# A four-block mixer on one core: ScalarE makes the decays of two token tiles in the even step, with one Exp over both, and the square and high part of z stand in front of them

## The reference, cut to what matters

```python
hBC = silu(conv(proj))                       # x, B and C
dt = softplus(dt + dt_bias)
A_cumsum = cumsum(A * dt)                    # per head, within a chunk
Lmat = exp(segment_sum(Ac))                  # exp(A_cumsum[l] - A_cumsum[s]), 0 above the diagonal
Gm = einsum('bclhn,bcshn->bclsh', C, B)
Y_diag = einsum('bclsh,bcshp->bclhp', Gm * Lmat, x * dt)
...
y = Y_diag + Y_off + D * x
z = y * silu(gate)                           # the norm's root is applied after the sum
out = z * norm_w @ out_proj_w.T
```

## Time and profile before

| what | value |
|---|---|
| median of three executions | 1733.1 us |
| the profiled execution's own time | 1734.61 us |
| its span, first to last instruction | 1732.9 us |
| TensorE busy | 97% |
| VectorE busy | 70% |
| ScalarE busy | 73% |
| GpSimd busy | 44% |
| mean granted TensorE clock | 0.989 of full speed |

### The profile page before, as it was taken

The page is one execution under the profiler, slowest core; times in us unless marked ns, Lnnn a source line. Parts: engine busy times, 40 slices in busy tenths (PEclk is TensorE's granted clock), DMA queues, the critical chain, the costliest instruction groups (busy, mean ns, idle before and its releaser), DMA issues.

```text
span 1732.9 us, 27059 instructions
## 1 busy us (share of the span) xinstructions
PE 1679.2 (97%) x9568; PEld 1388.4 (80%) x9568; DVE 1204.7 (70%) x1846; ACT 1265.2 (73%) x2171; POOL 754.7 (44%) x792
## 2 busy tenths in 40 slices
PE   6998898899999999999999999999999999999999
PEld 4877677788888888888888888888888888888777
DVE  4565685667776677668676767676767676767784
ACT  4332148887888778878888888788887888788851
POOL 3543122444444444544454444444444445345570
PEclk9999999999999999999999999999999999999999
DMA  4310225323233323232423232323233333332311
GB/s 164 116 68 1 73 68 156 102 86 112 86 113 96 109 89 112 87 117 73 127 89 104 75 110 101 102 95 110 88 104 94 110 98 106 93 108 77 107 68 49
DMA packets 98565, 166.47 MB, mean 96 GB/s; under 512 B 11616, under 2 KB 49888, under 8 KB 96768
## 3 DMA queue, kind: packets, MB, share of 16 engines
q1 hardware_dynamic: 98432, 164.75, 29.8%
HBM read 158.43 MB, written 6.29 MB: 95 GB/s over the span
## 4 chain that ended last, share of the span: by engine, by line
PE 80%; DVE 5%; ACT 2%; issue 1%; DVEq 0%; ACTq 0%
PE bank L210 14%; PE bank L212 14%; PE bank L211 14%; PE bank L1949 7%; PE bank L1950 7%; PE bank L1915 7%; PE bank L1953 7%; PE bank L1935 4%; PE bank L1901 3%; PE bank L1999 1%; DVE m_xc L1609 1%; DVE m_y L1688 1%; ACT m_mt L1365 1%; DVE m_y L1678 1%; DVE m_gate L1609 0%
## 5 line engine op out<-in xcount | busy, mean ns | idle before, releaser
L210 PE MATMUL bank<-xh,w_h 128*128 128x512 f32 x1152 | 463.2, 402 | 4.3 <-DVE m_xc L1609 3.8
L212 PE MATMUL bank<-xh,w_l 128*128 128x512 f32 x1152 | 452.4, 393 | 0.0
L211 PE MATMUL bank<-xl,w_h 128*128 128x512 f32 x1152 | 449.2, 390 | 0.0
L1273 POOL TENSOR_TENSOR m_z_l<-m_zg,m_z_h 128x512 fp32r<-128x512 f32 x128 | 175.2, 1369 | 514.1 <-ACT m_z_h L1413 514.1
L1365 ACT ACTIVATE m_mt<-m_mt,m_unit 128x128 f32<-128x128 f32 x1024 | 312.2, 390 | 0.0
L1255 POOL TENSOR_TENSOR w_l<-w_raw,w_h 128x512 fp32r<-128x512 f32 x144 | 187.2, 1300 | 247.4 <-ACT w_h L1332 247.4
L1620 DVE TENSOR_TENSOR x<-x,bank 128x512 f32<-128x512 f32 x128 | 87.6, 684 | 248.5 <-PE bank L1953 248.5
L212 PEld LDWEIGHTS bank<-xh,w_l 128*128 128x128 f32 x1152 | 216.6, 188 | 47.6
L1609 DVE SCALAR_TENSOR_TENSOR m_xc<-bank,m_par_conv,m_xc 128x1020 f32<-128x1020 f32 (+2 forms) x192 | 244.4, 1273 | 14.8 <-ACT m_xc L1344 10.2
L210 PEld LDWEIGHTS bank<-xh,w_h 128*128 128x128 f32 x1152 | 217.2, 189 | 46.0 <-issue 5.7
L211 PEld LDWEIGHTS bank<-xl,w_h 128*128 128x128 f32 x1152 | 217.6, 189 | 41.8
(11 more groups left out here) (277 smaller groups left out, 2846.3 us busy)
## 6 DMA issues: line engine op xcount, KB each, us to landing
m_mt<-ncs_rows SPq DMA_DIRECT2D x128, 512.0 KB, 4.6
w_raw<-w_in SPq DMA_DIRECT2D x144, 256.0 KB, 2.9
m_wo_raw<-w_out_in SPq DMA_DIRECT2D x64, 256.0 KB, 4.0
m_e<-ecs_rows SPq DMA_DIRECT2D x128, 128.0 KB, 3.5
a_wo_raw<-wo_in SPq DMA_DIRECT2D x8, 1024.0 KB, 4.8
x<-x_in SPq DMA_DIRECT2D x8, 256.0 KB, 5.1
a_wq_raw<-wq_in SPq DMA_DIRECT2D x8, 256.0 KB, 4.1
x_saved<-x SPq DMA_DIRECT2D x1, 2048.0 KB, 8.4
```

Source lines behind the costliest of these rows:

```text
L210: nc.tensor.matmul(out, ah, bh, start=first, stop=False)
L211: nc.tensor.matmul(out, ah, bl, start=False, stop=False)
L212: return nc.tensor.matmul(out, al, bh, start=False, stop=last)
L1273: nc.gpsimd.tensor_tensor(z_l[:, s % 2, :, :], zg[:], f(z_h[:, s % 2, :, :]), ALU.subtract).then_inc(zl_ready, 1)
```

## The change

`decay(s)` becomes `decays(s)`. It makes the tables of tiles s and s+1: sixteen Relu, then one Exp over both, 128x2048. It is called in even steps only, with s+2. And `square_and_high(s-1)` now stands in front of it; in the lead's last step `decay(16)` and `decay(17)` become one call in the lead's step 14. In the last group's steps 8 to 15, `square_and_high` stays behind the decays.

```diff
-            def decay(g, s):
-                g, s = g + s // STEPS, s % STEPS
+            def decays(g, s):
+                g, s = normal(g, s)
                 half, t = divmod(s, NT)
-                act.wait_ge(rows_loaded[s % ROW_BUFS], (g * (STEPS // ROW_BUFS) + (s // ROW_BUFS + 1)) * 16)
                 act.wait_ge(unit_loaded[half], (g + 1) * 16)
-                for h in range(UH):
-                    own_row = unit[:, half, NT * UH + t * UH + h:NT * UH + t * UH + h + 1]
-                    last = nc.scalar.activation(mt[:, s % ROW_BUFS, h, :], mt[:, s % ROW_BUFS, h, :], ACT.Relu,
-                                                bias=own_row)
-                last.then_inc(clamped, 1)
-                act.wait_ge(clamped, at(g, s))
-                slot = mt[:, s % ROW_BUFS, :, :]
-                nc.scalar.activation(slot, slot, ACT.Exp, scale=-1.0).then_inc(decay_ready, 1)
+                for i in range(2):
+                    row = s % ROW_BUFS + i
+                    act.wait_ge(rows_loaded[row], (g * (STEPS // ROW_BUFS) + (s // ROW_BUFS + 1)) * 16)
+                    for h in range(UH):
+                        col = NT * UH + (t + i) * UH + h
+                        last = nc.scalar.activation(mt[:, row, h, :], mt[:, row, h, :], ACT.Relu,
+                                                    bias=unit[:, half, col:col + 1])
+                last.then_inc(clamped, 2)
+                act.wait_ge(clamped, at(g, s + 1))
+                rows = mt[:, s % ROW_BUFS:s % ROW_BUFS + 2, :, :]
+                nc.scalar.activation(rows, rows, ACT.Exp, scale=-1.0).then_inc(decay_ready, 2)
...
-                if ahead(kind, s + 2) and not (kind == "lead" and s == STEPS - 1):
-                    decay(g, s + 2)
+                if paired(kind, s):
+                    for made in made_in(kind, s):
+                        square_and_high(g, made)
+                if s % 2 == 0 and ahead(kind, s + 2):
+                    decays(g, s + 2)
...
-                if kind == "lead" and s == STEPS - 1:
-                    decay(g, s + 2)
-                if paired(kind, s):
-                    for made in made_in(kind, s):
-                        square_and_high(g, made)
```

## The result

The changed kernel takes **2006.7 us** (median; 2001.5 to 2008.5) against 1733.3 us for the kernel before on the same chip: 1.157 times as long, interval [1.156, 1.159]. The loss is 273 us. The prediction had the sign and about half of the size: 1874 us, with a range that ended at 1905.

A forecast was written before the change was run, and what follows sets the result against it. TensorE, 97% busy, was taken as the bound. Stalls of 94 us in six middle groups, 9 in the first, 10 and 5 in the last made 118; with 22 for the clock, onto 1734.6, this gave 1874 us, range 1800 to 1905.

The forecast's parts named there:

- T + 12.4: When the paired decays are ready, counted from TensorE's start T of an even step, which lasts 8.7 us.
- step 3 of the sum: Steps 10 to 13: LATE evict and taps follow decays and Silu; the next projection stalls 2.2 us, twice a group.
- fit: Steps 14, 15 and 0 of a group: the later decays were claimed to cause no stall there.
- Step 2, the loop and turn(8): Steps 2 to 7: ScalarE-VectorE loop of 21.9 us against TensorE's 20.4, ending late at turn(8); loss 8.7 us a group.
- the last link alone: Decays and Silu of tile 5 ahead of turn(8): 5.9 us lost even with no loop.
- the milder rival: Sooner y and z or TensorE's own stalls reset the loop; turn(8) loses 5.9; about 1812 us; chance 0.17.
- Steps 1 and 3: Stalls for z_h in steps 1 and 9, 1.2 us, and for LATE tiles in steps 10 to 13, 2.2; each twice.
- the sum of the stalls: All forecast stalls over middle, first and last groups, without the clock: 118 us.
- The ends: First group's z_h wait and its slow matmuls go, -5 us; last group's step 8 wait grows from 1.97 to 5.
- The clock: Slow matmuls behind stalls: 12 us for eight at turn(8), 10 for fourteen of 2.2 us, half charged.
- The heavier loss: GpSimd's split or the clock adds to each stall, all groups; about 1940 us; chance 0.08.
- the rival at 1680: ScalarE's 11.8 us less work in each of eight groups makes the kernel faster, 1680 us; chance 0.01.

The follow-up runs named there:

- run 7: The changed kernel with the even step's mask behind the odd step's add_out, and add_out ahead of the LATE taps in steps 10 and 12: 1908.7 us.
- run 4: The changed kernel with the pair of decays ahead of square and high part, the pairing alone: 1889.4 us.
- run 8: The kernel before, with square and high part ahead of the decay in step 1 of the first group only: 1730.3 us.
- run 1: The changed kernel with the even step's mask moved behind add_out of the following odd step: 1935.6 us.
- run 2: The changed kernel with both masks made at the end of the odd step: 1935.3 us.

## Why the prediction was half right

**ScalarE's own numbers held.** Exp 1.913 us for 1.94; 62 loads for 64; 84 us less busy time for 80; the Exp's end at T + 12.0 for T + 12.4. That all of the saving was covered by TensorE held too.

**What failed: "the mask on VectorE" and all behind it.** The prediction says that "behind the mask on VectorE" stands "all of the next step; TensorE waits for both", and then followed only y, z and the taps of that queue. The instruction directly behind the mask, add_out, was counted for its 0.6 us and never asked who waits for it: the sum has no term for `across`. By the prediction's own figures: mask from T + 12.4, 1.1, add_out 0.6, so add_out over at T + 14.1; `across` of the odd step wants the bank at 8.72 for the step and about 2.5 for the turn and the diagonal part, T + 11.2. That is a stall of 2.9 us in steps 1, 3, 5 and 9. In steps 11 and 13 add_out stands behind the LATE taps, which by step 3 of the sum end at T + 19.8: over at T + 20.4, where `across` wants it at 14.2 + 2.5 = T + 16.7, a stall of 3.7. Over the groups, 30 x 2.9 + 14 x 3.7 = 139 us, from numbers that were all there. Measured: 138.3 us, the seven short waits of step 15 included. For steps 14, 15 and 0 the sentence "fit" was nearly right: only those waits of 0.5 us stand there.

**Step 2, the loop and turn(8).** 8.7 us a group were forecast, and 5.5 measured at turn(8), near the "5.9 for the last link alone". In the changed kernel the stalls at `across` push TensorE back and so reset the loop, as the milder rival had it: the Exp ends at T + 12.0 in each of steps 0, 2, 4 and 6. With them gone (run 7) the loop is there as forecast. TensorE's starts of steps 2, 4 and 6 and its turn(8), then ScalarE's Exp of the three steps:

```profile
908.47 0.60 PE L1907 MATMUL bank<-ident,m_xc 128*128 128x128 f32 x4
...
929.27 0.60 PE L1907 MATMUL bank<-ident,m_xc 128*128 128x128 f32 x4
...
950.25 0.60 PE L1907 MATMUL bank<-ident,m_xc 128*128 128x128 f32 x4
...
968.06 1.11 PE L1907 MATMUL bank<-ident,m_xc 128*128 128x128 f32 x4 [7.28 <-ACT m_xc L1356]
```

```profile
919.39 1.91 ACT L1374 ACTIVATE m_mt<-m_mt 128x2048 f32<-128x2048 f32 x1
...
941.21 1.92 ACT L1374 ACTIVATE m_mt<-m_mt 128x2048 f32<-128x2048 f32 x1
...
963.73 1.91 ACT L1374 ACTIVATE m_mt<-m_mt 128x2048 f32<-128x2048 f32 x1
```

The Exp ends at T + 12.8, 13.9 and 15.4, and from one end to the next are 21.8 and 22.5 us, where 21.9 was forecast. From T(2) to turn(8) the view of busy time by stretch has, for run 7:

```profile
908.47:968.06 59.59, 50.77 (x282) 40.62 (x280) 43.06 (x58) 44.14 (x80) 25.62 (x30) 0.97 0.24 73
```

That is 59.6 us where 58.5 was forecast and 49.7 stood before, with 8.8 us of idling against a forecast loss of 8.7. The wait at turn(8) itself is 7.3; the rest of the lateness is paid on the way, in short waits in steps 3, 5 and 6. So the loop was priced rightly, and in the changed kernel another stall hid a third of it.

**Steps 1 and 3.** The 1.2 us for z_h in steps 1 and 9 and the 2.2 for the LATE tiles do not appear in the changed kernel: the stall at `across` comes earlier in the same steps and covers them. In run 7 they are there. In steps 1 and 9 a middle group waits 0.65 and 0.86 us for z_h and each time 0.66 for GpSimd's part of z, 1.3 and 1.5 together (1.2 forecast). In step 11 the projection waits 2.5 us for the LATE tile's taps (the row with `m_gate`), in step 13 1.75 (in the row with `m_xc`), 2.1 on average (2.2 forecast). Of the rows above, 4.8 us for z_h are the last group's wait, and 5.3 of the 25.2 lie ahead of the first group, where 3.8 stood before. Not in the sum are seven waits of 0.8 us for VectorE's y in step 14, 5.7 in all. In all, run 7 idles 1896.3 - 1716.2 = 180.1 us, 126 more than before, where the sum of the stalls was 118.

**The ends.** The first wait for z_h went, as forecast; the one in the last group's step 8 grew from 1.97 to 4.76 (5 forecast).

**The clock.** 22 us were charged, 91 came. It is the count above all that was off: 1.5 us was charged for each of 8 stalls and half of it for 14. The waits of 0.5 us in step 15 have no slow matmuls behind them (behind the one at 1132.72 the 512-column matmuls start at 1133.92, 1134.15 and 1134.38), so the 91.3 us belong to the other 44 + 8 stalls, 1.8 each, a little over the 1.5 that was read from the earlier trace rows. For stalls of about 2.2 us half of it was charged; run 4 has TensorE busy 40.2 us longer over 53 such stalls, 0.76 each, which is that half. In run 7, without the stalls at `across`, TensorE is busy 37 us longer than before.

**The rivals.** None of them had the measured time. The heavier loss (1940) named the right kind of event, "steps 14 and 0 no longer fit: 5 us more a group", without its cause and in the wrong steps, and was still short. The rule that the Trainium skill gives ("ScalarE: Activation LUTs", Rules for kernel authors), to group by table set, was the ground for the rival at 1680: here 62 loads fewer ahead of Exp and Silu and 84 us less busy time went with 273 us lost. The drain of 1.38 us that the same page ("What ACT_TABLE_LOAD costs") adds to a switch shows in no row either: the load at 1015.02 takes 1.28 us and the Silu starts at 1016.31, 0.01 us behind it.

## What to carry to other kernels

When an instruction on an in-order queue becomes later, list what stands behind it there, and for each of those who waits for it, the semaphores that only give a buffer back included: the costliest wait here was for a bank that two unrelated matmul groups share. Merging work to save busy time on an engine that is not the bound moves the first half of the result to the end of the merged work, so compare that end with every consumer's due time before counting what was saved. Price a new stall on TensorE with the slow matmuls behind it: the 52 long stalls here cost 1.8 us each beside the wait. And do not take the sum of one kind of wait for what its removal wins: of 138 us of waits at `across`, 83 came up again elsewhere.

## What the hardware showed beyond that

Filling stalls with useless matmuls pays: 1312 turns of the identity, for the larger part in time in which TensorE would have waited (130 of 153 us), took 51 us off a kernel with no wait removed. A shorter stall is not surely slow behind: after 2.70 us at 960.88 in run 4 the matmuls follow at 0.23 us, after 1.84 us in run 8 they slow to 0.43 from the fourth on. Between such stalls the mean is what can be planned with, 0.76 us for each of 2.2 us in run 4, not the single case. VectorE's mask became longer by itself, 1262 to 1397 ns on average over the same 128 instructions. Its mean goes with its place in the queue: 1283 in run 1, 1583 in run 2, 1403 in run 4, 1251 in run 7. In the trace of the changed kernel the 41 masks that run beside a GpSimd instruction take 1.61 us on average and the others 1.30. That GpSimd's work is the cause is not shown: no run here moves it alone.
